# Cross-attention block on one core: two halves of the tokens with loops, or all tokens in one pass with keys and values kept in DRAM

## What is computed

```
for layer in (1, 2):
    h = layer_norm(x) * scale + offset
    q = h @ wq + bq                       # 16 heads of 128
    k = [ctx @ wk + bk ; bias_k]          # 256 keys of the batch and one more
    v = [ctx @ wv + bv ; bias_v]
    x = x + softmax(q k' / sqrt(128)) v @ wo + bo
h = layer_norm(x) * scale + offset
x = x + gelu(h @ w_fc1 + b_fc1) @ w_fc2 + b_fc2     # 2048 wide
```

## Time and profile before

| | |
|---|---|
| three runs | 2546.78, 2548.98 and 2550.6 us, median 2548.98 us |
| profiled execution | 2550.43 us |
| its span, first to last instruction | 2548.4 us |
| its mean granted TensorE clock | 0.984 of full speed |
| DMA, whole program | 105.48 MB read, 4.19 MB written |

### The profile page before, as it was taken

The page is one execution under the profiler, slowest core; times in us unless marked ns, Lnnn a source line. Parts: engine busy times, 40 slices in busy tenths (PEclk is TensorE's granted clock), DMA queues, the critical chain, the costliest instruction groups (busy, mean ns, idle before and its releaser), DMA issues.

```text
span 2548.4 us, 41898 instructions
## 1 busy us (share of the span) xinstructions
PE 2422.2 (95%) x13840; PEld 2101.8 (82%) x13840; DVE 1752.9 (69%) x3076; ACT 910.9 (36%) x2142; POOL 668.1 (26%) x427
## 2 busy tenths in 40 slices
PE   7999999999999999889999999999999999997998
PEld 5888888887888888768878888888888888886787
DVE  5777777678776776765567666777876677777555
ACT  3433333344333333411144333334343334333110
POOL 3322222223222222233312222222322222223322
PEclk9999999999999999989999999999999999999999
DMA  3111111111111111111301111111011111110111
GB/s 132 38 38 37 37 37 37 41 38 38 39 37 37 37 37 41 34 33 49 134 34 38 38 37 45 37 37 41 30 38 38 40 42 37 37 41 27 40 49 58
DMA packets 37507, 110.74 MB, mean 43 GB/s; under 512 B 4272, under 2 KB 5168, under 8 KB 37424
## 3 DMA queue, kind: packets, MB, share of 16 engines
q1 hardware_dynamic: 35312, 105.49, 12.3%
q10 hardware_dynamic: 2112, 4.19, 0.4%
HBM read 105.48 MB, written 4.19 MB: 43 GB/s over the span
## 4 chain that ended last, share of the span: by engine, by line
PE 65%; DVE 14%; issue 12%; ACT 6%; POOL 1%; DMA 1%; DVEq 0%; ACTq 0%; SPq 0%; POOLq 0%; PEldq 0%
PE U L489 17%; PE U L491 17%; PE U L490 17%; DVE probs L1027 3%; PE T L646 3%; ACT probs L805 3%; PE S L489 2%; DVE nm L1018 2%; PE S L491 2%; PE S L490 2%; ACT v_hi L798 2%; DVE v_lo L955 2%; DVE tmp L951 2%; DVE z L911 1%; PE O L491 1%
## 5 line engine op out<-in xcount | busy, mean ns | idle before, releaser
L1027 DVE TENSOR_SCALAR probs<-probs,rs 128x256 f32<-128x256 f32 x512 | 375.5, 775 | 9.0
L489 PE MATMUL U<-wos_hi,oT_hi 128*128 128x512 f32 x768 | 311.8, 406 | 11.5 <-DVE oT_lo L1095 6.8
L490 PE MATMUL U<-wos_lo,oT_hi 128*128 128x512 f32 x768 | 305.2, 397 | 0.0
L491 PE MATMUL U<-wos_hi,oT_lo 128*128 128x512 f32 x768 | 305.2, 397 | 0.0
L489 PE MATMUL U<-hT_hi,wqs_hi 128*128 128x512 f32 x768 | 302.7, 394 | 0.0
L490 PE MATMUL U<-hT_lo,wqs_hi 128*128 128x512 f32 x768 | 300.1, 391 | 0.0
L491 PE MATMUL U<-hT_hi,wqs_lo 128*128 128x512 f32 x768 | 299.9, 390 | 0.0
L489 PE MATMUL U<-wvs_hi,cT_hi 128*128 128x256 f32 x1024 | 297.9, 291 | 0.0
L490 PE MATMUL U<-wvs_lo,cT_hi 128*128 128x256 f32 x1024 | 290.0, 283 | 0.0
L805 ACT ACTIVATE probs<-S,nm 128x257 f32<-128x257 f32 x512 | 238.5, 473 | 143.8 <-DVE nm L1018 139.5
L491 PE MATMUL U<-wvs_hi,cT_lo 128*128 128x256 f32 x1024 | 289.9, 283 | 0.0
(11 more groups left out here) (101 smaller groups left out, 5406.7 us busy)
## 6 DMA issues: line engine op xcount, KB each, us to landing
raw_vq<-wa SPq DMA_DIRECT2D x49, 512.0 KB, 3.3
raw_ok<-wb SPq DMA_DIRECT2D x48, 512.0 KB, 4.5
raw_ok<-wk SPq DMA_DIRECT2D x33, 512.0 KB, 3.3
raw_vq<-wv SPq DMA_DIRECT2D x33, 512.0 KB, 3.3
raw_vb<-vrow SPq DMA_DIRECT2D x33, 256.0 KB, 3.5
c<-ctx_in SPq DMA_DIRECT2D x8, 512.0 KB, 7.6
x<-x_in SPq DMA_DIRECT2D x8, 512.0 KB, 8.5
out<-x ACTq DMA_DIRECT2D x4, 1024.0 KB, 5.4
```

What stands on the lines that cost most here:

```text
L489: pe.matmul(o, lhs[0], rhs[0], start=start, stop=False)
L490: pe.matmul(o, lhs[0], rhs[1], start=False, stop=False)
L491: return pe.matmul(o, lhs[1], rhs[0], start=False, stop=stop)
L1027: ins = dve.tensor_scalar(probs[:, r, qt, 0:256], probs[:, r, qt, 0:256], rs[:, r, qt:qt + 1], None, ALU.mult)
```

## The change

The halves, the four kinds of bodies and the hardware loops go. Everything is written out for each engine, over lists that are made once (`front_order`, `slot_order`, `last_order`).

- **Front.** For each of 8 groups of four heads (layer 1, then layer 2), all keys and values of all 2048 tokens are projected: 16 key units (one head, 512 tokens) and 16 value units (128 tokens, the 512 value columns of four heads). Each has 12 matmuls of 512 columns. ACT and DVE write the two parts into one of four slots of `stage`, and SP stores the slot in DRAM (`kd`, `vd`). The 8 batches of L0 run between these units, batch e within group e, in the PSUM banks of `S`, `T` and `O`. Input `ctx` is loaded into `x` itself. The turned rows of `ctx` (`cT`) and later those of the layer norm (`hT`) share one region of 64 KB per partition for all 2048 tokens.
- **Attention.** 64 steps: 16 pairs of heads by 4 chunks of 512 tokens. A step has four slots, each one item (one head, one batch), and loads one block of keys and one of values from DRAM into double buffers. Each slot is `L` of the next item, `T` of this one, a unit, `P` of the previous item, a second unit. The units of a step are the next step's queries (slots 0 and 2, half a unit on each side of `P`) and four output tiles (slots 1 and 3). `PT` has two buffers now.
- **The division** is moved from DVE to ACT (`divided`: two ACTIVATE Copy with a scale from `rs`, after the `oT_hi` of the previous item); DVE only inverts the sums.
- **The normalised rows** `z` are made by POOL (`tensor_scalar`), not DVE, one chunk of 512 tokens at a time, spread over four steps with the transposes in slots 1 and 2.
- **MLP.** 32 steps (8 pairs of 128 hidden columns by 4 chunks) with two buffers `gT`, the next step's hidden units ahead of this step's outputs; the high part after gelu is written by ACT, not DVE.
- **Queues.** The five constants are loaded from ACT's queue. The output is stored from SP's, one tile of 128 rows at a time, as it is done.

The diff replaces nearly the whole body; this is its core.

```diff
-UNITS_A = [("q", 0, 0), ("q", 0, 1), ("k", 1, 0), ("k", 1, 1), ("v", 1, 0), ("v", 1, 1), ("q", 1, 0), ("q", 1, 1),
-           ("w", 0, 0), ("w", 0, 1), ("K", 0, 0), ("w", 0, 2), ("w", 0, 3), ("K", 0, 1), ("V", 0, 0), ("V", 0, 1),
-           ("w", 1, 0), ("w", 1, 1), ("w", 1, 2), ("w", 1, 3)]
+L0_PARTS = {1: ("pg", 0), 2: ("pg", 1), 3: ("th", 0), 5: ("M", 0), 7: ("WM", 0), 9: ("wy", 0), 10: ("wy", 1)}
+def front_order():
+    out = [("cT", 0, ch) for ch in range(CH)]
+    for e in range(GROUPS):
+        for i in range(16):
+            c, h = divmod(i, 4)
+            out.append(("K", e, c, h))
...
+        for t in range(TILES):
+            out.append(("V", e, t))
...
+            if e == GROUPS - 1:
+                if t % 4 == 3:
+                    c = t // 4
+                    if c == 1:
+                        out += [("q", 0, h, s) for h in range(2) for s in range(2)]
+                    out += [("Z", 0, c, ch) for ch in range(CH)]
+                if t == 9:
+                    out.append(("L", 0))
+def slot_order(s, j):
+    item = 4 * s + j
+    if j in (0, 2):
+        first, second = ([projection(s + 1, j // 2, half)] for half in range(2))
+    elif j == 1:
+        first, second = ([("w", s - 1, t)] if s else [] for t in (2, 3))
+    else:
+        first, second = ([("w", s, t)] for t in (0, 1))
+    out = [("L", item + 1)] if item + 1 < ITEMS else []
+    out += [("T", item)] + first
+    out += [("P", item - 1)] if item else []
+    out += second
+    if norm_at(s) and j in (1, 2):
+        out += [("Z", *norm_at(s), ch) for ch in (2 * j - 2, 2 * j - 1)]
+    return out
...
+        kd = nc.dram_tensor("kd", (HBODIES, CHUNKS, P, 2, 2, 516), F32, kind="Internal").ap()
+        vd = nc.dram_tensor("vd", (GROUPS, CHUNKS, P, 2, 2, 4, 256), F32, kind="Internal").ap()
...
+            def load_k(s):
+                if s > 1:
+                    sp.wait_ge(logit, 4 * (s - 2) + 4)
+                sp.dma_start(f(kbuf[s % 2][:]), kd[s // CHUNKS, s % CHUNKS]).then_inc(k_in[s % 2], 16)
...
+            def values(e, t):
+                if t == 0:
+                    for i in range(2):
+                        pe.wait_ge(split[i], 2 * e + 2)
+                o = take("V", e, t)
+                for ch in range(CH):
+                    mm = product(o, parts(cT, ch, slice(t * P, t * P + P)), parts(wvs, ch, slice(0, 512)), ch == 0, ch == CH - 1)
+                mm.then_inc(unit, 1)
...
+            for s, j in SLOTS:
+                J = 4 * s + j
+                if j % 2 and s + 1 < STEPS:
+                    queries(s + 1, j // 2)
...
+                turned_hi(J)
+                if J + 1 < ITEMS:
+                    exponentials(J + 1)
...
+                if J:
+                    weighted_hi(J - 1)
+                if J + 1 < ITEMS:
+                    divided(J + 1)
```

More of the change, by code:

```diff
@@ L68, in units_of @@
[L68 to L95, removed]
@@ new lines, in projected @@
+            def projected(what, s, h, half):
+                c = s % CHUNKS
+                if half == 0:
+                    if c == 0 and h == 0:
+                        pe.wait_ge(split[0], use(s // CHUNKS + (HBODIES if what == "f" else 0)) + 1)
+                    if h == 0 and what == "q" and s % (BODIES * CHUNKS) < CHUNKS:
+                        pe.wait_ge(free, UNIT["Z", s // (BODIES * CHUNKS), c, CH - 1] + 1)
+                    if h == 0 and what == "f" and s < CHUNKS:
+                        pe.wait_ge(free, UNIT["Z", LAYERS, c, CH - 1] + 1)
+                    take(what, s, h)
+                o = bank(what, s, h)
+                for ch in (2 * half, 2 * half + 1):
+                    mm = product(o, parts(wqs, ch, slice(h * P, h * P + P)), parts(hT, ch, columns(c)), ch == 0, ch == CH - 1)
+                if half == 1:
+                    mm.then_inc(unit, 1)
@@ new lines, in output @@
+            def output(what, s, t):
+                if s % CHUNKS == 0 and t == 0:
+                    pe.wait_ge(split[1], use(s // CHUNKS + (HBODIES if what == "W" else 0)) + 1)
+                if what == "w" and t in (0, 2):
+                    pe.wait_ge(o_done, 4 * s + t + 2)
+                if what == "W" and t == 0:
+                    pe.wait_ge(free, UNIT["f", s, 1] + 1)
+                o = take(what, s, t)
+                src = oT if what == "w" else gT[s % 2]
+                for h in range(2):
+                    mm = product(o, parts(src, h, slice(t * P, t * P + P)), parts(wos, h, slice(0, D)), h == 0, h == 1)
+                mm.then_inc(unit, 1)
@@ new lines, in _ @@
+            pe.wait_ge(ident_ready, 1)
+            for what, *a in EVERYTHING:
+                if what == "K":
+                    keys(*a)
+                elif what == "V":
+                    values(*a)
+                elif what == "Z":
+                    rows(*a)
+                elif what in ("q", "f"):
+                    projected(what, *a)
+                elif what in ("w", "W"):
+                    output(what, *a)
+                elif what == "L":
+                    logits(*a)
+                elif what == "T":
+                    turn(*a)
+                elif what == "P":
+                    weighted(*a)
+                else:
+                    first_attention(what, *a)
@@ new lines, in _ @@
+            for what, *a in FRONT:
+                if what == "K":
+                    keys(*a)
+                elif what == "V":
+                    values(*a)
+                elif what == "Z":
+                    rows(*a)
+                elif what == "q":
+                    if a[2] == 1:
+                        queries(*a[:2])
+                elif what == "L":
+                    exponentials(0)
+                    divided(0)
+                else:
+                    first_attention(what, *a)
@@ new lines, in _ @@
+            output("w", STEPS - 1, 1)
+            for what, *a in last_order():
+                if what == "P":
+                    weighted_lo(*a)
+                elif what == "Z":
+                    rows(*a)
+                elif what == "f" and a[2] == 1:
+                    hidden(*a[:2])
+                elif what in ("w", "W"):
+                    output(what, *a)
+                    if (what, *a) == ("w", STEPS - 1, 3):
+                        for t in range(4):
+                            stats_of(STEPS - 1, t)
+                        moments(LAYERS, CHUNKS - 1)
```

1433 lines of the change are left out of this document (657 added, 776 removed).

## The result

The changed kernel takes 2438.63 us (median of 4 runs, 2435.99 to 2444.21) where the kernel before takes 2548.14 us on the same chip. The ratio is 0.957, with a 95% interval of 0.955 to 0.959: 110 us less. The forecast was 2422 us, 17 us too low; the range held the time. The profiled execution has a span of 2434.1 us.

What follows compares the result with a forecast made beforehand. PE was taken as the bound, busy 2422.2 of 2548.4 us. Its work of 2371 us plus 10 + 5 + 2 + 12 + 4 + 4 + 8 + 6 for starts, seams and other losses gave 2422 us; range 2398 to 2485.

Steps and rivals of the forecast that it cites:

- PE's work: Whole program: PE's matmuls and transposes, priced by distances between starts, sum to 2371 us.
- The plain slot: Attention: one item's PE work plus two half units takes 4.64 us, with 0 us of stalls.
- The slot's chain: Attention slot: ACT's `oT_hi` and two divisions end at 5.0 us, needed by 5.26; slack 0.25 us.
- The rival of a late ScalarE: Every attention slot: each `T` comes 0.3 us late, 77 us in all, 2499 us; chance 0.12.
- Stores: Front: 528 KB stored each 2.75 us, with weights 220 GB/s; hidden behind PE by four staging slots.
- The rival of stores in series: Front: stores don't overlap, 3.3 us each, 218 us more, 2640 us; chance 0.06.
- the seams: Attention steps with layer norm work: ACT has 2.8 us more in two slots; 1.5 us a step, 12 us.
- POOL late at the seams: Layer norm steps: rows at 2.4 us on POOL, queued with bias and splits, cost 32 us; 2460 us; chance 0.08.
- The first logits: Front to attention: PE waits at `L` of item 0 for the first block of keys, 5 us.
- The start: Program start: keys start at 12 us, after ctx, wk and the split, with 10 us idle.
- the end: Program end: a last tile's sum and a 256 KB store, 4 us.
- The step that was wrong in cause: Kernel before, attention bodies: PE's stop at `P` is a 0.75 us wait for `PT_lo`; about 1.1 us idle a body.

## Why the prediction was right, and where it was off

**PE's work** was the right term to build on: 2371 us forecast. The plain slot was put at 4.64 us; these four are from the kernel after:

```profile
1500.59 0.60 PE L642 MATMUL T<-ident,probs 128*128 128x128 f32 x4
1505.22 0.60 PE L642 MATMUL T<-ident,probs 128*128 128x128 f32 x4
1509.85 0.60 PE L642 MATMUL T<-ident,probs 128*128 128x128 f32 x4
1514.45 0.60 PE L642 MATMUL T<-ident,probs 128*128 128x128 f32 x4
```

4.63, 4.63 and 4.60 us. The values at 512 columns stand 0.227 us apart, the lower bound and not my 0.231. L0 among the front's units was dearer in my sum than on the chip. A group of the front from 138.83 to 234.28 us is 95.4 us; 32 units of 12 x 0.227 are 87.2 of it, and eight such groups are 763 us, where I had 785. Six of the eight groups take just this; the first takes 13 us more, with the turned rows of `ctx` and 9 us of waits for them.

**The slot's chain** held. ACT's division takes 0.50 us, next to my 0.47, and PE's wait for `probs` in `T` is 1.7 us in the whole program. The rival of a late ScalarE did not come, and the division's place proved to be free.

**Stores** were hidden as forecast. The rival of stores in series is refuted by the doubled stores: 20 us, not 794.

**The step that failed in size is the seams**: "I give 1.5 us a step, 8 steps, 12 us". The five steps around the first seam take 36 us more than plain ones, of which 16 transposed blocks are 7 to 9 us of PE; so some 28 us are lost at one seam, and the stretch at the second adds 12 us of idle PE. Three terms were short. A row tile on GpSimd was taken at 1.4 us, inside its bounds of 0.5 and 2.4, and is 2.08 at the seams; with it a chunk takes 1.0 + 8.3 = 9.3 us, so no cover is left. ScalarE's 2.8 us more in a slot were counted against PE's time only. That they cost 9 us at the first seam is shown by the short activations; that it happens through the four banks, which go to the transposes in slots 1 and 2 and come back one slot late, is my reading of the order and not tested. And VectorE's low part of each transposed block was put at nothing, though GpSimd's bias additions hold it for up to 5.2 us and PE waits 4.3 us for one. The rival "POOL late at the seams" was part of this. The faster front (22 us) hid most of the error in the sum, which is luck.

**The first logits** were put at 5 us and cost 8.2, because the block, queued with three stores, lands in 7.1 us and not in the 5.4 of an output store. The start (10.6 us idle before the first key matmul, about 10 forecast) was as forecast, and the end took 3 us of 4.

**The step that was wrong in cause** stands where I explained the kernel before. I put the stop at `P` down to `PT_lo` in VectorE's queue, and of the 375 us of division I said only that it left VectorE further from the bound. I did not ask why an instruction of 0.35 us had a mean of 0.775. The same oversight sits in the row that I took for the normalised rows: VectorE's 1.35 us is a mean over 48, of which 36 are held by GpSimd, and a tile takes 0.54 alone. The runs show that 64 to 69 of the 110 us come from there: the old order has GpSimd split a weight in the middle of each body, 163 times, beside VectorE's divisions, and the stops, their tails and restarts are 1.6 us a body. In the new order there are 80 splits, and with the division on VectorE only 32 of 512 take over 0.5 us. This could be had without the rest of the change. Of the rest, the wider values are worth 23 us and the loops 7. The 10 to 15 us that are left I put down to half as many seams and starts; no run tests that, and since the parts overlap, this is an account and not a proof. The sum came right because it was built from PE's distances between starts, in which all stops of before vanish whatever their cause.

## What to carry to other kernels

When a group's mean is far above its shortest instructions, look at what the other engines run beside the long ones before placing the work elsewhere: here it was GpSimd's elementwise instructions, and either a shorter one or another engine for VectorE's part took away 64 to 69 us. Then look again in the new kernel: there the same collision had moved to other instructions. Build a forecast for a bound engine from the distance between starts. Where work is spread over an order written by hand, write each engine's queue out for the irregular steps as well; they carried most of the error, while the plain steps came out to 1%.

## What the runs showed of the hardware

- Some VectorE instructions from SBUF to SBUF are held while GpSimd runs a two-input TENSOR_TENSOR or a CAST, and end 0.1 to 0.6 us after it: a division of 0.35 us takes 2.56 beside a 1024-column subtraction, a row tile of 0.54 takes 1.40 to 1.48 in the median beside a bias addition, and the subtraction for `hT` of 0.69 takes up to 5.22 beside several additions in a row.
- Others are not. The reciprocal of 128x2 takes 0.17 us also inside such an instruction (66 of them in the kernel before), and VectorE's work on PSUM shows no stretch (`PT_lo` has a mean of 0.69 us in every kernel).
- GpSimd's TENSOR_SCALAR of the rows holds a division little: with the division on VectorE 24 meet one, their median is 0.36 us and the longest 0.77, and 16 of them start and end inside it.
- The same 128x512 row normalisation takes 0.54 us on VectorE when alone and 2.08 on GpSimd, where a two-input addition of the same size has a mean of 1.44 in the kernel before.
- The turns of the hardware loops over plain bodies cost PE nothing that shows here (149.45 and 149.46 us for the same stretch of the MLP, with its loop and written out); writing out all loops gains 7 us, at starts and seams.
- Stores of 1 KB and 2 KB runs into DRAM from one queue hold 376 GB/s together with the weight loads, and single ones of 512 KB land in 3.1 to 3.2 us while the next is on its way.
